# A four-stage image network on one core: group variance, pooled features and the first normalisation made by GpSimd, one input load issued later

## The reference

```python
def reference(x, ...):
    x = x + L0_conv(gn(x), ...)
    x = x + L1_conv(gn(x), ...)
    x = x + L2_conv(gn(x), 8)
    x = x + L3_conv(gn(x), ...)
    return x
```

## Time and profile before

| | us |
|---|---|
| median of 3 runs | 767.77 |
| lowest, highest | 767.4, 771.08 |
| the profiled execution, its own time | 776.6 |
| its span | 774.7 |
| TensorE busy | 624.3 (81%) |
| VectorE busy | 611.5 (79%) |
| ScalarE busy | 563.9 (73%) |
| GpSimd busy | 200.6 (26%) |
| mean granted TensorE clock | 0.945 |

### The profile page before, as it was taken

The page is one execution under the profiler, slowest core; times in us unless marked ns, Lnnn a source line. Parts: engine busy times, 40 slices in busy tenths (PEclk is TensorE's granted clock), DMA queues, the critical chain, the costliest instruction groups (busy, mean ns, idle before and its releaser), DMA issues.

```text
span 774.7 us, 13144 instructions
## 1 busy us (share of the span) xinstructions
PE 624.3 (81%) x4142; PEld 188.2 (24%) x4142; DVE 611.5 (79%) x1100; ACT 563.9 (73%) x1081; POOL 200.6 (26%) x291
## 2 busy tenths in 40 slices
PE   0351845899798999899889988999899789889992
PEld 0211211223222222233223322322232223222220
DVE  1352785598959998989988998879887889769993
ACT  0112110689868998899889988998898968898882
POOL 1302024402541235213521353125300630230000
PEclk9985886899989999999999999999999999999996
DMA  5759499407985739254834574455640560065002
GB/s 98 139 91 178 101 189 211 73 14 146 170 192 97 173 88 206 66 112 107 183 87 109 110 164 107 109 112 132 141 109 3 125 146 1 2 146 125 1 1 54
DMA packets 72865, 85.53 MB, mean 110 GB/s; under 512 B 8674, under 2 KB 58354, under 8 KB 72818
## 3 DMA queue, kind: packets, MB, share of 16 engines
q1 hardware_dynamic: 68096, 78.58, 47.6%
q10 hardware_dynamic: 4722, 6.34, 4.5%
HBM read 9.14 MB, written 8.39 MB: 23 GB/s over the span
## 4 chain that ended last, share of the span: by engine, by line
PE 36%; DVE 22%; ACT 17%; DMA 8%; issue 8%; SPq 6%; POOL 1%; ACTq 1%; DVEq 0%; POOLq 0%
PE pz L756 19%; PE pc L702 8%; ACT u L610 7%; DVE g L991 6%; ACT u L618 6%; PE pc L733 6%; DMA win<-y 5%; DVE u L987 3%; ACT u L615 2%; DVE bn L923 2%; DVE box_sum L1024 2%; DMA xs<-in_x_dram 2%; DVE xs L974 2%; PE po L763 2%; DMA stack<-near_sum 2%
## 5 line engine op out<-in xcount | busy, mean ns | idle before, releaser
L610 ACT ACTIVATE u<-pz 128x512 f32<-128x512 f32 x472 | 275.4, 603 | 93.3 <-PE pz L756 92.7
L756 PE MATMUL pz<-g,wT 64*64 64x512 f32 x1536 | 296.7, 614 | 18.7 <-DVE g L991 15.1
L991 DVE SCALAR_TENSOR_TENSOR g<-u,pz 128x512 f32<-128x512 f32 x384 | 250.3, 681 | 62.1 <-ACT u L618 58.7
L618 ACT ACTIVATE u<-u 128x512 f32<-128x512 f32 x472 | 289.6, 643 | 1.3
L756 PEld LDWEIGHTS pz<-g,wT 64*64 64x64 f32 x1536 | 80.5, 132 | 212.2 <-issue 210.4
L733 PE MATMUL pc<-win,t 64*32 64x512 f32 x1392 | 98.0, 667 | 27.0 <-DMA win<-y 16.0
L702 PE MATMUL pc<-box_sum,box_mat 128*128 128x512 f32 x180 | 90.9, 621 | 12.3 <-DVE box_sum L1024 12.3
L923 DVE BATCH_NORM_STATS2 bn<-xs 128x6 f32<-128x512 f32 (+1 forms) x128 | 82.8, 682 | 22.0 <-DMA xs<-in_x_dram 20.2
L468 POOL TENSOR_TENSOR stat<-stat,con 128x1 f32<-128x1 f32 x32 | 22.5, 704 | 272.9 <-DVE stat L943 272.9
L991 DVE SCALAR_TENSOR_TENSOR g_last<-u,pz 128x512 f32<-128x512 f32 x128 | 82.5, 680 | 9.1 <-ACT u L618 7.1
L756 PE MATMUL pz<-stack,wT 64*64 64x512 f32 x512 | 81.7, 620 | 9.5 <-DMA stack<-near_sum 4.2
(11 more groups left out here) (87 smaller groups left out, 366.6 us busy)
## 6 DMA issues: line engine op xcount, KB each, us to landing
stack<-near_sum SPq DMA_DIRECT2D x90, 192.0 KB, 4.0
win<-y SPq DMA_DIRECT2D x56, 260.0 KB, 4.2
win<-y SPq DMA_DIRECT2D x56, 195.0 KB, 4.3
out_dram<-xs SPq DMA_DIRECT2D x8, 1024.0 KB
stack<-box_sum SPq DMA_DIRECT2D x60, 128.0 KB, 3.8
xs<-in_x_dram SPq DMA_DIRECT2D x7, 1024.0 KB
stack<-near_sum SPq DMA_DIRECT2D x30, 128.0 KB, 3.4
win<-y ACTq DMA_DIRECT2D x8, 260.0 KB, 8.2
```

The costliest lines, as they stand in the source:

```text
L610: act.activation(u[:, m, :], pz[:, m, :], ACT.Relu, scale=-1.0, bias=0.0).then_inc(relu_done, 1)
L618: act.activation(u[:, m, :], u[:, m, :], ACT.Exp, scale=-1.0).then_inc(exp_done, 1)
L756: last = pe.matmul(pz[to, m, :], wT[rows, l, rows], src, start=True, stop=True)
L991: dve.scalar_tensor_tensor(out=elus(l)[:, m, :], in0=u[:, m, :], scalar=-1.0, in1=pz[:, m, :], op0=ALU.add, op1=ALU.max).then_inc(g_writte ...
```

## The change

Three things are done. The negated variance and the variance plus epsilon, two VectorE instructions for each sample and stage, become two GpSimd instructions at the head of `scales`. `pool_features` becomes GpSimd's, behind `scales` of stage 0 and so a round's length earlier than before. And for samples 3 to 7 `normal0` is made by GpSimd with two tensor-tensor instructions for each chunk, behind a wait for the round's fourth `box_scan` and in front of `mix`; samples 0 to 2 stay with ScalarE in the start-up. Beside it, in round 1 SyncE issues `load(5)` behind `windows0(3)` and no longer in front of it. Semaphore waits follow: `logits` waits for the PSUM reader by name, `softmax_in(0)` for the set-up.

```diff
--- before.py
+++ after.py
@@ -178,6 +178,7 @@
         y3_written = sem("y3_written")
         y3_edges = sem("y3_edges")
         y2_scaled = sem("y2_scaled")
+        y0_scaled = sem("y0_scaled")
         box_rows = sem("box_rows")
         near_pairs_done = sem("near_pairs_done")
         near_pairs_first = sem("near_pairs_first")
@@ -403,13 +404,13 @@
                     sp.nop(nofuse=True)
                     windows1(sp, t + 1, range(2), True)
                 first = isinstance(t, int) and t == 1
-                if first:
-                    sp.wait_ge(x_loaded, loaded(4))
-                    load(5)
                 if has(t + 2):
                     sp.wait_ge(conv_mm[0], 2 * (t + 2))
                     sp.nop(nofuse=True)
                     windows0(sp, t + 2, range(2), True)
+                if first:
+                    sp.wait_ge(x_loaded, loaded(4))
+                    load(5)
                 if has(t):
                     stacks(sp, t, 0)
                     stacks(sp, t, 1)
@@ -462,6 +463,11 @@
 
             def scales(i, k):
 
+                pool.wait_ge(stat_step[k], i * STAT + Q + 3)
+                pool.tensor_tensor(nv[k][:, 0:1], gs[k][:, 0:1], gs[k][:, 0:1], ALU.mult).then_inc(stat_step[k], 1)
+                pool.wait_ge(stat_step[k], i * STAT + Q + 4)
+                pool.nop(nofuse=True)
+                pool.tensor_scalar(nv[k][:, 1:2], gs[k][:, 1:2], nv[k][:, 0:1], EPS, ALU.subtract, ALU.add).then_inc(stat_step[k], 1)
                 pool.wait_ge(stat_step[k], i * STAT + STAT)
                 if k < 2 and not (isinstance(i, int) and i == 0):
                     pool.wait_ge((y0_written, y1_written)[k], (Y0, 2)[k] * i)
@@ -469,6 +475,19 @@
                 pool.wait_ge(norm_step[k], i * NORM + 1)
                 pool.nop(nofuse=True)
                 pool.tensor_scalar(st[k][:, 1:2], gs[k][:, 0:1], st[k][:, 0:1], -1.0, ALU.mult, ALU.mult).then_inc(norm_step[k], 1)
+
+            def pool_features(i):
+
+                pool.wait_ge(norm_step[0], i * NORM + NORM)
+                if isinstance(i, int) and i == 0:
+                    pool.wait_ge(s_channel, 16 * N_CHANNEL_DMA)
+                else:
+                    pool.wait_ge(route_step, i * ROUTE)
+                pool.nop(nofuse=True)
+                pool.tensor_scalar(pooled[:, :], gs[0][0:C, 2:3], st[0][0:C, 0:1], st[0][0:C, 1:2], ALU.mult, ALU.add).then_inc(route_step, 1)
+                pool.wait_ge(route_step, i * ROUTE + 1)
+                pool.nop(nofuse=True)
+                pool.tensor_scalar(fcp[:, :], fcT[:, :], pooled[:, 0:1], None, ALU.mult).then_inc(route_step, 1)
 
             def mix(i):
 
@@ -496,6 +515,23 @@
                 pool.wait_ge(y2_scaled, Q * i + c + 1 - Q)
                 pool.tensor_tensor(rows, rows, two, ALU.add).then_inc(y2_written, 1)
 
+            def normal0(i, c):
+
+                if c == 0:
+                    pool.wait_ge(norm_step[0], i * NORM + NORM)
+                    pool.wait_ge(win0_in, WIN0 * i)
+                rows = blocks(y0, c)[:, :, 1:W + 1]
+                one, two = (st[0][:, n:n + 1].unsqueeze(2).to_broadcast([P, KB, W]) for n in range(2))
+                pool.tensor_tensor(rows, sample(i, c).rearrange("p (k w) -> p k w", w=W), one, ALU.mult).then_inc(y0_scaled, 1)
+                pool.wait_ge(y0_scaled, Q * i + c + 1 - 3 * Q)
+                pool.tensor_tensor(rows, rows, two, ALU.add).then_inc(y0_written, 1)
+                if c % 2:
+                    half = slice((c - 1) * KB, (c + 1) * KB)
+                    pool.wait_ge(y0_written, Y0 * i + 2 * c)
+                    pool.nop(nofuse=True)
+                    pool.tensor_copy(y0[:, half, 0:1], y0[:, half, 2:3]).then_inc(y0_written, 1)
+                    pool.tensor_copy(y0[:, half, W + 1:W + 2], y0[:, half, W - 1:W]).then_inc(y0_written, 1)
+
             def edges3(i):
 
                 pool.wait_ge(conv_mm[2], Q * i + Q)
@@ -521,6 +557,9 @@
                 if has(t + 1):
                     scales(t + 1, 1)
                 if has(t + 2):
+                    pool.wait_ge(box_rows, Q * t + Q)
+                    for c in range(Q):
+                        normal0(t + 2, c)
                     mix(t + 2)
                     spread(pool, t + 2)
                 if has(t):
@@ -530,19 +569,23 @@
                         near_sums(t, c)
                 if has(t + 3):
                     scales(t + 3, 0)
+                    pool_features(t + 3)
                 if has(t + 1):
                     scales(t + 1, 2)
                     for c in range(Q):
                         normal2(t + 1, c)
 
             scales(0, 0)
+            pool_features(0)
             mix(0)
             spread(pool, 0)
             scales(0, 1)
             scales(1, 0)
+            pool_features(1)
             mix(1)
             spread(pool, 1)
             scales(2, 0)
+            pool_features(2)
             scales(0, 2)
             scales(1, 1)
             edges3(0)
@@ -552,6 +595,7 @@
             mix(2)
             spread(pool, 2)
             scales(3, 0)
+            pool_features(3)
             scales(1, 2)
             for c in range(Q):
                 normal2(1, c)
@@ -643,8 +687,6 @@
                         if has(t + 2):
                             if at == 5 + first:
                                 softmax_exp(t + 2)
-                            if at in (6, 7, 8, 9):
-                                normal0(t + 2, at - 6)
 
             for c in range(Q):
                 normal0(0, c)
@@ -680,8 +722,10 @@
                     last = pe.matmul(psm[:, 2:3], const("chan"), ms[k][:, 0:1], start=True, stop=True)
                 last.then_inc(sums_mm[k], 1)
 
-            def logits(i):
+            def logits(i, freed=None):
                 pe.wait_ge(route_step, i * ROUTE + 2)
+                if freed:
+                    pe.wait_ge(stat_step[freed[1]], freed[0] * STAT + Q + 3)
                 pe.matmul(psm[:, 8:8 + EXPERTS], const("ones", C), fcp[:, :], start=True, stop=True).then_inc(logits_mm, 1)
 
             def box_band(i, c, d):
@@ -815,7 +859,7 @@
                         if at == 3 + first and has(t + 1):
                             group_sums(t + 1, 1)
                         if at == 4 + first and has(t + 2):
-                            logits(t + 2)
+                            logits(t + 2, (t + 1, 1))
                         if at == 9 and has(t):
                             group_sums(t, 3)
                         if at == 10 and has(t + 3):
@@ -936,21 +980,11 @@
                 n = 3 if k == 0 else 2
                 dve.wait_ge(sums_mm[k], i + 1)
                 dve.tensor_copy(gs[k][:, 0:n], psm[:, 16 * k:16 * k + n]).then_inc(stat_step[k], 1)
-                dve.wait_ge(stat_step[k], i * STAT + Q + 3)
-                dve.scalar_tensor_tensor(out=nv[k][:, 0:1], in0=gs[k][:, 0:1], scalar=gs[k][:, 0:1], in1=gs[k][:, 1:2],
-                                         op0=ALU.mult, op1=ALU.subtract).then_inc(stat_step[k], 1)
-                dve.wait_ge(stat_step[k], i * STAT + Q + 4)
-                dve.tensor_scalar(nv[k][:, 1:2], nv[k][:, 0:1], -1.0, EPS, ALU.mult, ALU.add).then_inc(stat_step[k], 1)
-
-            def pool_features(i):
-
-                dve.wait_ge(norm_step[0], i * NORM + NORM)
-                dve.tensor_scalar(pooled[:, :], gs[0][0:C, 2:3], st[0][0:C, 0:1], st[0][0:C, 1:2], ALU.mult, ALU.add).then_inc(route_step, 1)
-                dve.wait_ge(route_step, i * ROUTE + 1)
-                dve.tensor_scalar(fcp[:, :], fcT[:, :], pooled[:, 0:1], None, ALU.mult).then_inc(route_step, 1)
 
             def softmax_in(i):
                 dve.wait_ge(logits_mm, i + 1)
+                if isinstance(i, int) and i == 0:
+                    dve.wait_ge(setup_dve, 1)
                 dve.tensor_tensor(logit[:, :], psm[:, 8:8 + EXPERTS], fcb[:, :], ALU.add).then_inc(route_step, 1)
                 dve.wait_ge(route_step, i * ROUTE + 3)
                 dve.tensor_reduce(nmax[:, :], logit[:, :], AX.X, ALU.max, negate=True).then_inc(route_step, 1)
@@ -1117,8 +1151,6 @@
                             if at in (10, 11):
                                 normal3(t, at - 10)
                         if has(t + 2):
-                            if at == 3 + first:
-                                pool_features(t + 2)
                             if at == 4 + first:
                                 softmax_in(t + 2)
                             if at == 6 + first:
@@ -1153,7 +1185,6 @@
             merge_stats(0, 0)
             group_var(0, 0)
             setup_channels()
-            pool_features(0)
             softmax_in(0)
             setup_natural()
             setup_transposed()
@@ -1171,13 +1202,11 @@
             stats_of(1, 0, range(Q))
             merge_stats(1, 0)
             group_var(1, 0)
-            pool_features(1)
             softmax_in(1)
             stats_of(2, 0, range(Q))
             merge_stats(2, 0)
```

(1 more changed line is left out.)

## The result

The changed kernel takes 764.65 us (median of 11 runs, 760.67 to 766.82) against 770.02 for the kernel before on the same chip (11 runs, 766.07 to 772.32): a ratio of 0.9934, 95% interval 0.9913 to 0.9954. That is faster, by 0.5 to 0.9%, where 1.0% was forecast.

A forecast was written before the change was run, and what follows sets the result against it. ScalarE was taken to pace slots 4 to 10, VectorE close behind; elsewhere TensorE waits for VectorE's evacuations. Terms -4.5 - 0.3 - 5.2 + 2.0 = -8.0 us took the 767.8 median to 759.8; range 748 to 770.

The forecast's parts named there:

- Part 1: Slots 4 to 10, rounds 1 to 5: normal0 leaving ScalarE gains 0.6 us a round, bounds 0 and 3.7.
- relief in full: Rival: in slots 4 to 10 VectorE's work slides into its gaps, gaining 4.7 to 5.1 us a round; 741; chance 0.17.
- Part 2: Slots 9, 14, 3 and 12: variance and features leaving VectorE gain 0.8 us a round, bounds 0 and 1.9.
- Part 3: GpSimd takes the work in idle time; VectorE meeting it costs 0.5 us a round, bounds 0 and 1.0.
- slower: the shared port: Rival: in slots 6 to 9 VectorE instructions wait out GpSimd's, +1.7 us a round net; 772.8; chance 0.12.
- Steady rounds: Rounds 1 to 5: -0.6 - 0.8 + 0.5 = -0.9 us each, -4.5 in all.
- Part 4: Round 1, slot 12 to next slot 0: load(5) behind the windows removes TensorE's wait; gain 5.2 us, bounds 0 and 5.5.
- the load gives it back: Rival: the moved load delays sample 1's stacks for round 2's slot 0, so round 1's gain is lost; 765.0; chance 0.14.
- The step from profile to median: Whole kernel: the profiled run's 8.8 us above the 767.8 median carries over, so 768.6 becomes 759.8.
- Part 5: Start-up: sample 0's four serial stages each wait 0.5 us longer for scales; +2.0 us, bounds 0 and 2.8.
- Rounds 6 and 7: Round 6, with three group_vars and no normal0, was forecast to gain 0.3 us.

The follow-up runs named there:

- sections 2 and 3: On the kernel before: load(5) moved behind windows0(3), 1.0015; with that move, only normal0 on GpSimd, 0.9922, or only variance and features there, 0.9987.

## Why the prediction was right or wrong

The direction, the mechanism in the steady rounds and the range were right; the size was not. Of the 4.9 us between 759.8 and 764.65, 2.6 are the sum (-8.0 against -5.4 by the medians), and 2.3 the level of the kernel before, 770.02 here and 767.77 in the three runs shown.

- **Part 1, ScalarE is relieved: right.** Forecast -0.6 a round, measured -0.66 in slots 8 to 11. The reason given, that VectorE is next, holds: of the two gaps of slot 8, 0.64 us, 0.25 is left, those of slot 10 stay, and the gain is in slot 9, behind the evacuation that TensorE waits for (from TensorE's layer of slot 9 to that of slot 10 it is 5.50 us before and 4.94 after). The rival *relief in full* (4.7 a round) is out.
- **Part 2, VectorE is relieved: right in size, one place instead of four.** Forecast 0.3 in slot 9, 0.4 before slot 15, 0.1 in slot 3, sum 0.8; measured 0.61, all before slot 15. There the term of 0.4 was too small. Its 0.38 us was read in slot 9 and without the wait behind the copy of the sums; from that copy to the evacuation of slot 14 it was 0.67 and is 0.07. Slots 3 and 9 gave nothing, with normal0 on either engine.
- **Part 3, GpSimd takes it: right, with a smaller price.** Forecast +0.5 for the port meeting, within 0 to 1.0; measured +0.23, as the three-column tensor-scalar took 0.68 us beside GpSimd's tensor-tensors (0.23 alone). By the rule of the Trainium skill ("SBUF — State Buffer", "SBUF: two separate sides") one instruction of 1.04 us is the most it can wait beside normal0, which with its own 0.23 makes 1.27. The trace agrees: in rounds 1 to 5 it takes 0.28, 0.69, 0.68, 0.68 and 0.41. Its longest, 1.24, is in the start-up beside a neighbour sum of 1.18, as before the change. No join, statistic or evacuation grew, so the rival *slower: the shared port* is out. Taking the meeting away gave the 0.23 back, and 0.1 more in slots 8 to 11.
- **Steady rounds: -0.9 forecast, -1.04 measured.** -0.66 + 0.23 - 0.61 = -1.04, with each term isolated by a run. That the sum is nearer than its terms is luck: 0.27 too much for the port and 0.19 too much for VectorE's relief nearly cancel.
- **Part 4, load(5): wrong, and this is the step that failed.** "Gain 5.2; bounds 0 and 5.5" took the excess of one execution (25.67 us for slots 12 to 15 of round 1, against 20.45) for what the kernel costs. The mean of three profiles is 22.3, an excess of 1.9, so this term alone made the sum 3.3 too large. It also put the gain down to the load's place. By itself the move gains nothing (1.0015): the wait for the windows goes, and one of 2.21 for the stacks comes in its place. Taken out of the changed kernel it is not missed (0.9946). What the runs show instead: slots 12 to 15 of round 1 take 19.35 in the changed kernel, 3.0 less than the mean. 0.45 of that is VectorE's relief (19.80 with normal0 alone), the rest the DMA waits that are gone. With the load behind the windows they are gone because GpSimd's normal0 lets the load go 5 us earlier, so that the stacks behind it are in time (sections 2 and 3); with the load in front, one profile shows a wait of 0.17 us more, and why so little is open.
- **The rival *the load gives it back*** names 765.0, nearest of all to the 764.65 measured, and that is luck: its late stacks are in the runs with the load moved and normal0 on ScalarE, and not in the changed kernel.
- **The step from profile to median: wrong.** "A difference of this kind carries over": the profiled run was 8.8 us above the median partly because of the wait that I then took off the median. Slots 12 to 15 of round 1, 25.67 us in that profile, took 19.79 and 21.48 in the next two. With the mean of the three (22.3) the gain there is 3.0; with the one profile it was 6.3. Those 3.4 us are more than the whole error of the sum; part of it is made up by slots 4 to 11 of round 1, which gained more than a steady round.
- **Part 5, the start-up: not resolved.** +2.0 forecast, of 0.5 per chain; the chain grew by 0.32, so 1.3 for four. Profiles give +2.3 against the mean of three and +0.9 over all fourteen, with a spread of 4 us between profiles of one kernel.
- **Rounds 6 and 7:** -0.3 forecast, +0.2 measured, below the spread between profiles (148.57 to 150.60).

What stays open: why the windows behind the load land at 74.3, 70.8 and 72.0 us by the clock of round 1 in three executions of the kernel before, and at 69.0 in the changed kernel with the load in front. Their source is not what differs, as their second half is issued 55.2 to 56.7 us after the round's start in all four; the time from issue to landing does, and no run says what sets it.

## What to carry to other kernels

A wait that appears once in a program, in a fill or drain round, is worth its mean over several executions, while one in a loop's steady state can be read from one profile to 0.1 us; take two or three profiles before a one-off wait enters a sum, and don't subtract it from a median that never held it. Relief of the pacing engine is worth the idle time of the engine behind it, and that is read in the timeline slot by slot, not from a busy share of 99% (TensorE's here held its waits for the joins); the price of moved work is read from the narrow SBUF instructions of VectorE that fall beside it. Once an engine is relieved, fill it again in small pieces, and look where its idle time lies: half of a normalisation gained 0.3 us a round, the whole lost 0.7.

## What was not expected of the hardware

- With the load ahead of them the first five windows DMAs take 9.18 to 10.46 us to issue, without it 3.53 to 4.18, and the last two land 8.5 to 12.3 us after their issue, without it 3.1 to 3.4 where normal0 is ScalarE's. That repeats in every profile, while the wait seen by TensorE goes from 0 to 3.98.
- GpSimd multiplies a 128x1 tensor by a tensor in 0.19 us and copies 128x8 in 0.20; the power of the same size takes 0.57. I had put the multiply at 0.27 to 0.57 and the copies at 0.3. Beside VectorE's scan the same multiply took 1.18 us, as it sat the scan out.
- VectorE's tensor-scalar of three columns takes 0.68 us beside GpSimd's tensor-tensors and 0.23 elsewhere: the meeting makes a narrow instruction three times as long. Over the changed kernel:

```profile
L997 DVE TENSOR_SCALAR route<-ex,nmax x8: 228/546/1241, 27.6 to 493.2; 128x3 f32<-128x3 f32 x8
```

- ScalarE does the second half of normal3 (128x1024, SBUF to SBUF) beside GpSimd's neighbour sums in 1.24 to 1.28 us, and the first, where GpSimd is idle, in 1.26. VectorE does a half in 0.81 us where GpSimd is idle and in 1.76 beside the sums: the faster engine alone is the slower one there.
